# Correlation products of 2x16 pixels on four column tiles, with operands kept in bands of two rows column by column

## What is computed

```python
def layer(feature, conv_w, conv_b):              # feature: group norm of x, 512 channels
    norm = jnp.sqrt(jnp.sum(feature * feature, axis=1, keepdims=True))
    fn = feature / jnp.maximum(norm, 1e-12)
    fp = jnp.pad(fn, ((0, 0), (0, 0), (2, 2), (2, 2)))
    corr = jnp.stack([jnp.sum(fp[:, :, r:h + r, cc:w + cc] * fn, axis=1)
                      for cc in range(5) for r in range(5)], axis=1)
    cat = jnp.concatenate([feature, corr], axis=1)
    return jax.nn.relu(jnp.einsum('oc,bchw->bohw', conv_w, cat) + conv_b[None, :, None, None])

x = x + layer(group_norm(x), w0, b0)
x = x + layer(group_norm(x), w1, b1)
```

## Time and profile before

| | |
|---|---|
| median of 3 runs | 527.68 us (525.36 to 530.27) |
| the profiled execution's own time | 526.55 us, of which the span is 524.8 us |
| TensorE matmul busy | 470.0 us (90%) |
| VectorE busy | 370.0 us (71%) |
| ScalarE busy | 276.4 us (53%) |
| GpSimd busy | 127.6 us (24%) |
| DMA | 71.76 MB, mean 137 GB/s |

### The profile page before, as it was taken

The page is one execution under the profiler, slowest core; times in us unless marked ns, Lnnn a source line. Parts: engine busy times, 40 slices in busy tenths (PEclk is TensorE's granted clock), DMA queues, the critical chain, the costliest instruction groups (busy, mean ns, idle before and its releaser), DMA issues.

```text
span 524.8 us, 9885 instructions
## 1 busy us (share of the span) xinstructions
PE 470.0 (90%) x3880; PEld 259.5 (49%) x3880; DVE 370.0 (71%) x868; ACT 276.4 (53%) x370; POOL 127.6 (24%) x179
## 2 busy tenths in 40 slices
PE   0557597679996999999998999999999999999996
PEld 0443445364643646464553646464646455464442
DVE  4788896768967687786869495868878695623322
ACT  1443455447383665839383755657493848433222
POOL 3534420131330313131220313131312212140400
PEclk9978898879998999999999999999999999999999
DMA  8271263542220465447566673232322325463432
GB/s 297 108 252 51 87 201 117 138 117 54 82 82 8 118 213 164 128 158 242 203 213 223 208 267 117 55 115 55 86 85 50 114 72 176 146 189 106 148 115 107
DMA packets 50876, 71.76 MB, mean 137 GB/s; under 512 B 12276, under 2 KB 37932, under 8 KB 50830
## 3 DMA queue, kind: packets, MB, share of 16 engines
q1 hardware_dynamic: 41038, 62.21, 35.5%
q0 software_dynamic: 9792, 8.92, 7.1%
HBM read 34.97 MB, written 33.59 MB: 131 GB/s over the span
## 4 chain that ended last, share of the span: by engine, by line
PE 60%; DVE 18%; ACT 7%; DMA 6%; issue 4%; POOL 3%; SPq 1%; DVEq 0%; ACTq 0%; POOLq 0%
PE conv_ps L567 42%; PE gram_ps L487 8%; DVE operands L837 4%; DVE stats L790 4%; PE conv_ps L576 4%; DMA vol<-corr_h 4%; ACT operands L661 3%; ACT v L667 3%; PE gram_ps L499 2%; DVE xs L920 2%; POOL v L430 2%; DVE operands L843 1%; DMA xs<-in_x_dram 1%; PE turn_ps L557 1%; POOL vol L293 1%
## 5 line engine op out<-in xcount | busy, mean ns | idle before, releaser
L567 PE MATMUL conv_ps<-operands,wh 128*128 128x512 f16 x1024 | 326.0, 383 | 0.3 <-DVE wl L908 0.3
L567 PE MATMUL conv_ps<-operands,wl 128*128 128x512 f16 x512 | 195.8, 382 | 0.0
L694 ACT ACTIVATE act_out<-conv_ps,bias,wdown 128x512 f32<-128x512 f32 x128 | 95.9, 772 | 133.9 <-PE conv_ps L576 125.1
L567 PEld LDWEIGHTS conv_ps<-operands,wh 128*128 128x128 f16 x1024 | 100.8, 98 | 122.4 <-issue 4.8
L837 DVE TENSOR_TENSOR operands<-v,operands 128x1024 f16<-128x1024 f32 x64 | 81.5, 1274 | 59.1 <-ACT v L667 53.9
L920 DVE TENSOR_TENSOR xs<-xs,act_out 128x512 f32<-128x512 f32 x128 | 85.9, 683 | 36.6 <-ACT act_out L694 36.3
L790 DVE BATCH_NORM_STATS2 stats<-xs 128x6 f32<-128x512 f32 x128 | 79.7, 678 | 5.5 <-DMA xs<-in_x_dram 5.5
L661 ACT ACTIVATE operands<-xs,affine 128x1024 f16<-128x1024 f32 x64 | 78.5, 1233 | 5.6 <-DVE affine L830 5.6
L567 PEld LDWEIGHTS conv_ps<-operands,wl 128*128 128x128 f16 x512 | 50.5, 99 | 57.9 <-issue 1.5
L487 PE MATMUL gram_ps<-operands 128*64 128x192 f16 x960 | 74.3, 252 | 2.1 <-ACT band L675 2.1
L293 POOL DMA_DIRECT2D vol<-corr_h x48 | 35.5, 747 | 166.3 <-DVE corr_h L859 166.2
(11 more groups left out here) (80 smaller groups left out, 257.5 us busy)
## 6 DMA issues: line engine op xcount, KB each, us to landing
xs<-in_x_dram SPq DMA_DIRECT2D x32, 512.0 KB, 6.3
out_dram<-xs SPq DMA_DIRECT2D x32, 512.0 KB, 3.0
band_dram<-band SPq DMA_DIRECT2D x64, 192.0 KB, 3.2
skew<-band_dram SPq DMA_DIRECT2D x64, 133.0 KB, 3.0
vol<-corr_h POOLq DMA_DIRECT2D x48, 50.0 KB, 2.7
rows_dram<-rows SPq DMA_DIRECT2D x32, 65.8 KB
rows_dram<-rows SPq DMA_DIRECT2D x32, 63.3 KB
mirror<-rows_dram POOLq DMA_DIRECT2D x14, 110.9 KB, 2.5
```

The source lines that it names most:

```text
L567: pe.matmul(conv_ps[:, g % 4, :], w[:, l, t, m * P:(m + 1) * P], opnd[:, u % RING, part, t, n * HALF:(n + 1) * HALF], start=(t == 0 and w ...
L694: act.activation(act_out[:, g % 2, :], conv_ps[:, g % 4, :], ACT.Relu, bias=bias[:, l, m:m + 1], scale=wdown[:, l, m:m + 1]).then_inc(relu, 1)
```

## The change

- The pixels of the operands (`opnd`, `v`, `half`, and with them `vol` and the convolution's output) are kept in another order: bands of two rows, within a band column by column, the two rows' pixels side by side. ScalarE, GpSimd and VectorE write or read through `by_rows` and `in_rows`: the innermost run on the permuted side has a step of two elements.
- A weight tile is 2x16 pixels: 32 columns, four column tiles. The moving side is a window of 3 bands (low part) or 2 bands (high part) by 18 columns by 2 rows: 108 or 72 columns. A unit has 4 x 2 x 8 x 4 = 256 matmuls; there are no fillers. The output of a tile is a window of 6x20, stored row by row, while the columns of a matmul come band by band, column by column, rows innermost: two columns that follow each other lie 20 elements apart, in PSUM words.
- All 8 blocks of a unit fit into two PSUM banks (4 x 120 elements each), which VectorE clears once at the start. The products of a unit are issued in one piece, a bank at a time; `average` stands behind them.
- ScalarE copies 2 banks of 480 elements in place of 4 of 384, both ahead of `deviations`. SyncE writes 8 transfers of 32x480 in place of 4 of 128x384, and reads 2 of 128x445 in place of 4 of 64x4x133; the read of a bank waits for that bank's writes alone. The zero pads in DRAM, and SyncE's wait for them, are gone. The first layer's weights are turned in `conv_ps`.

```diff
-    TILE = TROWS * WI
-    SPLIT = P // TILE
+    SPLIT = 4
+    TILE = P // SPLIT
+    TCOLS = TILE // TROWS
+    WROWS = TROWS + 2 * R
+    WCOLS = TCOLS + 2 * R
+    WINDOW = WROWS * WCOLS
...
+        def in_rows(a):
+            return a.rearrange("p (y e x) -> p y e x", e=TROWS, x=WI)
+        def by_rows(a):
+            return a.rearrange("p (y x e) -> p y e x", e=TROWS, x=WI)
...
+            def window_at(j, s, first, n):
+                left, right = columns(s)
+                at = gram_ps[s * TILE:(s + 1) * TILE, j // BANK_BLOCKS,
+                             j % BANK_BLOCKS * WINDOW:(j % BANK_BLOCKS + 1) * WINDOW]
+                at = at.rearrange("p (y e x) -> p y x e", x=WCOLS, e=TROWS)
+                shift = R - s % ACROSS * TCOLS
+                return at[:, first:first + n, left + shift:right + shift, :]
...
+            def bank_products(u, n, t):
+                for j in range(n * BANK_BLOCKS, (n + 1) * BANK_BLOCKS):
+                    for s in range(SPLIT):
+                        low_product(u, j, s, t)
+                    for s in range(SPLIT):
+                        last = high_product(u, j, s, t)
+                return last
...
-                pe.wait_ge(band_sb, PAIRS * u + p - 1)
-                for j in (p, p + FOLD):
+            def products(u):
+                pe.wait_ge(low, KT * (u + 1))
+                pe.wait_ge(halved, KT * (u + 1))
+                for n in range(BANKS):
+                    pe.wait_ge(band_sb, BANKS * (u - 1) + n + 1)
                     for t in range(KT):
-                        last = block_products(u, j, t)
-                last.then_inc(gram, 1)
+                        last = bank_products(u, n, t)
+                    last.then_inc(gram, 1)
...
-                    for p in range(PAIRS):
-                        products(k, p)
-                        if p == 1 and valid(k + 1):
-                            average(k + 1)
+                    products(k)
+                    if valid(k + 1):
+                        average(k + 1)
...
-                act.activation(opnd[:, u % RING, 0, t, :], xs[:, ring_slot(unit_batch(u)), t, :], ACT.Identity,
+                act.activation(by_rows(opnd[:, u % RING, 0, t, :]), in_rows(xs[:, ring_slot(unit_batch(u)), t, :]),
+                               ACT.Identity,
...
-                act.activation(act_out[:, g % 2, :], conv_ps[:, g % 4, :], ACT.Relu,
+                act.activation(in_rows(act_out[:, g % 2, :]), by_rows(conv_ps[:, g % 4, :]), ACT.Relu,
...
+            dve.memset(gram_ps[:, :, :], 0.0).then_inc(gram_clear, 1)
```

More of the change, by code:

```diff
@@ L196, in build @@
         band_sb = sem("band_sb")
-        band_out = sem("band_out")
+        band_out = [sem(f"band_out{n}") for n in range(BANKS)]
         skew_in = sem("skew_in")
@@ L370, in _ @@
             load(1)
-            pads()
             band_through_dram(0)
@@ L474, in filler @@
[L474 to L495, removed]
-                    below = opnd[:, u % RING, 0, t, (n + 1) * TILE:(n + 2) * TILE]
-                    moving = bass.AP(moving.tensor, moving.offset,
-                                     [list(moving.ap[0]), [below.offset - moving.offset, 2], [1, TILE]])
-                return pe.matmul(tile_at(u, n, R * WI, size), opnd[:, u % RING, 0, t, n * TILE:(n + 1) * TILE],
-                                 moving, start=False,
-                                 stop=(t == KT - 1 and (u > 0 or not opens(u, n))))
@@ L503, in block_products, with band_of, weights_at @@
[L503 to L508, removed]
-                for n in tiles:
-                    low_product(u, n, t)
-                for n in tiles:
-                    last = high_product(u, n, t)
+            def band_of(j, s):
+                return (j % HALVES * FOLD + j // HALVES) * SPLIT // ACROSS + s // ACROSS
+            def weights_at(u, j, s, t):
+                first = (band_of(j, s) * ACROSS + s % ACROSS) * TILE
+                return opnd[:, u % RING, 0, t, first:first + TILE]
@@ L513, in block_products @@
+            def bank_products(u, n, t):
+                for j in range(n * BANK_BLOCKS, (n + 1) * BANK_BLOCKS):
+                    for s in range(SPLIT):
+                        low_product(u, j, s, t)
+                    for s in range(SPLIT):
+                        last = high_product(u, j, s, t)
                 return last
             def first_products():
+                pe.wait_ge(gram_clear, 1)
                 for t in range(KT):
@@ L591, in _ @@
                 channels(0, g)
-            for p in range(PAIRS):
-                products(1, p)
+            products(1)
             average(2)
@@ L601, in _ @@
             turn(1)
-            for p in range(PAIRS):
-                products(2, p)
-                if p == 1:
-                    average(3)
+            products(2)
+            average(3)
             for g in range(4):
@@ L699, in _ @@
                 norm_tile(0, t)
-            for p in range(PAIRS):
-                band_out_of_psum(0, p)
+            for n in range(BANKS):
+                band_out_of_psum(0, n)
             for n in range(KT + 1):
@@ L848, in correlation @@
                 o, m, far, near = (framed(a[:, :])[:, :, 0:WI] for a in (own, mirror, rn_far, rn_own))
-                total = image(corr[:, :])
+                o_rows, m_rows = (a.rearrange("p (y e) x -> p y e x", e=TROWS) for a in (o, m))
                 wait_views(dve, k)
```

148 lines of the change are left out of this document (69 added, 79 removed).

## The result

| | before | after |
|---|---|---|
| median | 526.6 us (525.4 to 530.3) | 538.3 us (537.6 to 539.4) |
| ratio | | 1.018 [1.013, 1.023] |
| span of the profiled execution | 524.8 us | 536.0 us |
| up to the first product of round 5 | 175.2 | 174.7 |
| rounds 5 to 14 | 283.6 | 293.7 |

Slower by 1.8%; the forecast was 527 and no change. (The medians here are of four runs each. The quotient of the two medians alone would be 1.022, that of the spans 1.021; both lie inside the interval.) By the profiled executions the ten rounds lose 10.1 us, the end 1.7, and the start gains 0.5. Runs that were slow as a whole are left out of all times (one of e5 took 815.9 us, with a granted clock of 0.58).

What follows compares the result with a forecast made beforehand. TensorE, almost without pause, was taken as the bound, a second chain beside it. Eight rounds +3.2, rounds 7 to 9 -1.5, start -1.9: -0.2, so 526.3; the median 1.1 above the profiled execution gave 527, range 499 to 545.

Steps and rivals of the forecast that it cites:

- Products 4.9 us, convolution at 5.4: TensorE's round: products take 4.9 us, the convolution starts at 5.4 in place of 4.99, +0.4 in eight rounds; chance 0.42.
- the two reasons offered: For products at 4.9 us, not 2.5: only two column tiles run at once, or PSUM columns 20 words apart cost double.
- The rival of one matmul at a time: TensorE's 256 matmuls and as many weight loads are limited by hand-out: products 7.2 us, total 552; chance 0.20.
- The rival of the full rate, 502: Four column tiles run side by side at full rate: products 2.5 us, -25 us in all, total 502; chance 0.33.
- ScalarE's steps "at nothing": ScalarE's passes with steps of two elements were taken at the same cost per element, so nothing added.
- 0.5 of spare time: Second chain: correlations land 16.4 us behind the average and are wanted 16.9 behind it, leaving half a microsecond.
- The rival with doubled passes: ScalarE's four slab passes of 1.23 us double, adding 4.9 us, 4.4 in eleven rounds: near 575; chance 0.05.
- Average behind products, 0.5: The average, moved behind the products on TensorE, costs 0.5 us there; bounds 0.15 and 0.5.
- Rounds 7 to 9, -0.5 each: Rounds with image loads ahead of the correlations' landing gain 0.5 us each, -1.5 together; bounds -1.7 and +2.6 each.
- the forecast's 11.8: SyncE's queue: image loads go out near 11.8 us into the round in place of 12.5.
- the 12.7 us of waits for `vol`: TensorE's profiled wait total for the correlations, 12.7 us, which the prediction placed in rounds 7 to 9.
- Start, -1.9: Round 3: band copies come early, taking 1.9 us off the chain of ScalarE and VectorE; bounds 0 and -4.

Runs made afterwards that it cites:

- e5: The changed kernel with 64 small matmuls on zeros added at the start, while TensorE waits for the first image: 538.1 us, ratio 1.018 to the kernel before.
- e1: The changed kernel with column order kept in PSUM too, so products write runs of neighbouring columns: 538.3 us, ratio 1.016 to the kernel before.
- e13: The changed kernel with the first convolution group and the average between the two banks of products from unit 3 on: 541.5 us, ratio 1.022 to before.
- e10: The changed kernel, average between the banks, the first convolution group's twelve matmuls spread among the products from unit 3 on: 562.4 us, ratio 1.063 to before.
- e3: The changed kernel with ScalarE's and GpSimd's slab passes writing pixels in rows, without steps of two elements: 532.6 us, ratio 1.005 to before.
- e8: The changed kernel with VectorE's correlation moved ahead of the two low passes: 535.8 us, ratio 1.011 to the kernel before.

## Why the prediction was wrong

- **Products 4.9 us, convolution at 5.4: right** where nothing else happens (0.15 us for eight, 4.75 for all, 5.19 with the average). Of the two reasons offered, the stride in PSUM is the one: with neighbouring columns the rate doubles (e1). By the Trainium skill (Advanced Engine Details and Errata, section PSUM Cachelines) every two elements should lie together; the traces agree, 0.15 against 0.08.
- **The step that failed: the products were priced by columns and by matmuls, never by the instructions that have to be brought in.** The change doubles the products' instructions in the same 5 us, and no term of the sum stood for that. Rounds 5 to 14 have 8.7 us of gaps (0.3 of them behind the products of round 11), round 15 another 1.25. That they come from the supply of instructions is shown by their place (e5, each at a multiple of 256), by their growth with the rate (e1), and by their end when slower instructions stand between (e13, e10). The rival of one matmul at a time came nearest in spirit (it counted matmuls and weight loads), but its mechanism is wrong: between gaps a matmul follows each 18.6 ns, and each 10 in e1, against the 28 it took. The Trainium skill (Runtime: NRT & Kernel Launch, section Instruction fetch mechanics) calls the cost of crossing such a 16 KB block mostly hidden; here it was, while 256 instructions of products took 4.8 us (before), and it was not where two times 256 followed each other at 2.4 us each (gaps up to 1.9) or at 1.3 (up to 2.8).
- **The rival of the full rate, 502:** e1 has that rate and no gain: its -25 us lacked the same term.
- **ScalarE's steps "at nothing": mis-sized.** They are +24% and +7%, 0.75 us over the four passes between average and `vol`, against 0.5 of spare time. The rival with doubled passes had the mechanism at a size far too large. Their price: e3 is 5.2 us shorter in span, 1.7 before round 5 and 3.5 in rounds 5 to 14, where the gaps are nearly the same and the waits of the second chain are gone.
- **Average behind products, 0.5: mis-sized.** It costs 0.25 behind its products (386.28 to 386.53).
- **Rounds 7 to 9, -0.5 each: near in sum, and in that lucky.** Without their gaps the three take 86.4 us in place of 87.6, -1.1 against the forecast's -1.5; but round 7 gets longer (+0.7) and round 8 shorter (-1.5). Over 28.0 they lost 3.6 before; over 28.19 and their gaps they lose 1.9 now. The loads of round 8 go out 11.7 into the round, near the forecast's 11.8, with a gap of 1.8 among its products ahead of them. Rounds 6, 11 and 14 lose some 1.1 that they did not before: the spent spare time. One reading was wrong: the 12.7 us of waits for `vol` were put down to rounds 7 to 9, but 9.8 of them stand in rounds 1 and 2.
- **Start, -1.9: mis-sized, -0.5.** Round 4's products start 4.0 earlier (134.89), but TensorE's wait for VectorE in that round ends at 162.44 in place of 163.10, so the wait grows from 4.37 to 6.8 and the round by 3.5. The forecast saw that VectorE's chain is the bound there; it let the chain keep all of the 1.9, with ScalarE's steps at nothing. With plain passes (e3) the wait ends at 160.11, and round 5 starts 2.2 earlier than before.

The sum of rounds 5 to 14: products with average +0.19 in ten rounds, 1.9; gaps 8.7; waits of the second chain 3.1 in place of 3.6, -0.5. Together 10.1, as measured. Of the 1.7 at the end 1.25 is a gap. No run takes the gaps out and leaves all else as it is; that they cost 8.7 us follows from this sum, and from e8, where nine of the ten rounds are alike once their gap is taken off. How long a gap is depends on when its transfer starts: in after, 0.4 to 2.0 us after TensorE has begun the 256 instructions that stand ahead of the gap, then 0.9 to 1.4 for the transfer and 1.3 to 1.6 until work goes on, while those 256 last only some 2.4. In round 9, the longest, these are 2.0, 0.9 and 1.4. What stays open: why the transfer starts so late in some rounds; no run tells.

## What to carry to other kernels

When a change makes many small instructions of few large ones, price the stretch three times: by columns, by matmuls, and by instructions, with the densest stretch that the trace shows without a pause as the bound. A gain in one of the three is worth only what the next leaves. And where a wait is for another engine, ask whether the change makes that engine's work longer before counting a gain there. A row of waits is a total over the whole span: before a chain is blamed for it, read in which rounds the waits stand.

## What the runs showed that was not expected

- Where TensorE takes two times 256 instructions one after the other, each in 2.4 us, gaps of 0.4 to 1.9 us stand in most rounds; at 1.3 us each, gaps of mostly 2.0 to 2.8. Work resumes 1.2 to 1.6 us behind the transfer's end. One such stretch of 2.4 us with 2.8 us of few instructions behind it leaves none in ten of eleven rounds (e13).
- A product output whose columns lie 20 words apart in PSUM runs at half the rate (0.15 and 0.08 us for eight matmuls of 180 columns on each of four tiles). ScalarE reads PSUM in steps of two words without loss (L689: 770 ns; before, side by side, 772).
- A change from four column tiles to the whole array and back costs 0.2 to 0.3 us (e10).
- ScalarE writing 128x1024 in float16 in steps of two elements takes 1526 ns in place of 1233, in float32 1315; reading float32 from two rows in turn, 1459.
